# First layer's opening merged into its attention block, and the first group's row bound spread by a product with ones

## What is computed

```python
xn = layernorm(x, ln_x_g, ln_x_b)            # x: the context, 6404 rows
ln = layernorm(latents, ln_l_g, ln_l_b)      # latents: the (normed) residual, 1024 rows
q  = ln @ Wq
kv = concat([xn @ Wkv, ln @ Wkv])
qn, kn = rmsnorm(q, qn_g) * scale, rmsnorm(k, kn_g)
sim = where(mask, qn @ kn.T, max_neg)
out = softmax(sim) @ v @ Wout + bout
```

## Time and profile before

| | |
|---|---|
| median of three runs | 4295.99 us (4293.72 to 4296.5) |
| the profiled execution's own time | 4296.1 us |
| its span, first to last instruction | 4294.0 us |
| PE busy | 4024.4 us, 94% of the span |
| DVE busy | 3373.1 us, 79% |
| ACT busy | 3160.8 us, 74% |
| POOL busy | 417.7 us, 10% |

### The profile page before, as it was taken

How to read it: one execution, slowest core, us unless ns; L and a number is a source line. 1 busy time by engine, 2 the same in 40 slices (tenths; PEclk the granted TensorE clock), 3 DMA queues, 4 the chain that set the end, 5 groups by cost and what they waited for, 6 DMA issues and landing times. The chain is left out here.

```text
span 4294.0 us, 65601 instructions
## 1 busy us (share of the span) xinstructions
PE 4024.4 (94%) x25721; PEld 2648.7 (62%) x26161; DVE 3373.1 (79%) x5198; ACT 3160.8 (74%) x5109; POOL 417.7 (10%) x337
## 2 busy tenths in 40 slices
PE   3999999999999999999989799999999999999996
PEld 2666666666666666666657566666666666666664
DVE  5788888888887878878877677777777777777775
ACT  3888888888888888888864567676767676666662
POOL 3111111111111111111100000000000000000000
PEclk9999999999999999999989799999999999999997
DMA  1000000000000000000012000000000000000001
GB/s 40 1 1 16 1 5 13 1 17 1 5 13 1 17 1 6 11 1 18 1 34 92 5 1 17 1 17 1 17 1 5 13 3 15 1 16 1 15 1 44
DMA packets 29159, 50.25 MB, mean 12 GB/s; under 512 B 9118, under 2 KB 17574, under 8 KB 26790
## 3 DMA queue, kind: packets, MB, share of 16 engines
q1 hardware_dynamic: 26932, 45.85, 3.4%
q10 hardware_dynamic: 1922, 0.17, 0.0%
HBM read 45.15 MB, written 0.85 MB: 11 GB/s over the span
## 5 line engine op out<-in xcount | busy, mean ns | idle before, releaser
L824 DVE TENSOR_TENSOR a_probs_lo<-a_probs 128x1024 fp32r<-128x1024 f32 x1760 | 2126.2, 1222 | 562.3 <-ACT a_probs L637 253.4
L633 ACT ACTIVATE a_probs<-scores_ps,a_c_bias,a_k_rstd 128x512 f32<-128x512 f32 x1888 | 1311.9, 776 | 31.1 <-PE scores_ps L1180 30.8
L1205 PE MATMUL out_ps<-a_probs_lo,a_v 128*128 128x512 f32 x3520 | 1135.3, 443 | 0.0
L637 ACT ACTIVATE a_probs<-scores_ps,a_c_bias 128x1024 f32<-128x1024 f32 x816 | 867.7, 1112 | 113.4 <-PE scores_ps L1180 113.0
L1198 PE MATMUL out_ps<-a_probs,a_v 128*128 128x512 bf16 x3080 | 849.9, 389 | 85.2 <-issue 58.8
L1180 PE MATMUL scores_ps<-a_q_hi,a_k_hi 64*128 64x512 f32 x3520 | 790.9, 444 | 18.8 <-ACT a_probs L633 9.4
L1205 PEld LDWEIGHTS out_ps<-a_probs_lo,a_v 128*128 128x128 f32 x3520 | 658.7, 188 | 219.3 <-DVE a_probs_lo L824 0.5
L1180 PE MATMUL scores_ps<-a_q_lo,a_k_hi 64*128 64x512 f32 x3520 | 701.6, 393 | 0.0
L1180 PE MATMUL scores_ps<-a_q_hi,a_k_lo 64*128 64x512 f32 x3520 | 698.0, 391 | 0.0
L1198 PEld LDWEIGHTS out_ps<-a_probs,a_v 128*128 128x128 f16 x3520 | 272.4, 97 | 561.7 <-issue 304.8
L602 ACT ACTIVATE a_v<-proj_ps 128x256 f16<-128x256 f32 x448 | 172.2, 384 | 488.4 <-PE proj_ps L1112 488.2
(11 more groups left out here) (272 smaller groups left out, 3293.4 us busy)
## 6 DMA issues: line engine op xcount, KB each, us to landing
a_den<-a_inv_row SPq DMA_DIRECT2D x16, 1024.0 KB, 4.6
normed<-in_L_xattn_we_g SPq DMA_DIRECT2D x16, 256.0 KB, 2.8
m_gate_spread<-m_combine_row SPq DMA_DIRECT2D x8, 512.0 KB, 4.0
a_wkv_raw<-in_L_xattn_wkv_g SPq DMA_DIRECT2D x16, 128.0 KB, 2.1
a_wo_raw<-in_L_xattn_wo_g SPq DMA_DIRECT2D x16, 128.0 KB, 2.0
m_w_raw<-in_L_ffn_w1T SPq DMA_DIRECT2D x8, 256.0 KB, 4.3
m_w_raw<-in_L_ffn_w2T SPq DMA_DIRECT2D x8, 256.0 KB, 4.6
m_gate_spread<-m_combine_row SPq DMA_DIRECT2D x8, 256.0 KB, 5.8
```

The costliest lines, as they stand in the source:

```text
L633: ins = nc.scalar.activation(probs[:, pb, e * 512:(e + 1) * 512], scores[:, b, e * 512:(e + 1) * 512], ACT.Exp, bias=cbias[:, tile:tile + ...
L637: ins = nc.scalar.activation(probs[:, pb, :], scores[:, b, :], ACT.Exp, bias=cbias[:, 1:2] if last else cbias[:, 0:1])
L824: nc.vector.tensor_tensor(plow[:, idx % NPL, :], probs[:, idx % NB, :], p_hi[:, idx % NB], ALU.subtract).then_inc(plo_ready, 1)
L1205: nc.tensor.matmul(outs[:, e * 512:(e + 1) * 512], v32[:, c % 2, t, e, :], plow[:, idx % NPL, e * 512:(e + 1) * 512], start=False, stop=t ...
```

## The change

Layer 0's preparation block and the opening block of the kernel are gone; all their instructions now stand in the attention block's lists, woven into group 0's opening. The context is loaded in three parts (16, 20 and 15 tiles, a semaphore each) issued right behind X, the gates and the first weights, with nothing to wait for but the last four rows. It is placed in buffers that the steps use later (`probs`, `out_acc`); the transposed tiles go through a ring of five half-buffers instead of two, and their PSUM through four places. The latents' two low parts move from POOL to DVE. The order on each engine is written anew:

```diff
@@ DVE, layer 0 @@
+                    dve.wait_ge(B["loaded"], 48)
+                    ln_stats(dve, lstep, row_x, 0, QT, B["few"], var_ready, LATC)
+                    ctx_stats(0)
+                    ln_apply(dve, lstep, row_x, row_z, 0, QT, B["few"], rstd_ready, 1, LATC)
+                    ln_stats(dve, lstep, row_z, 0, QT, B["few"], var_ready, LATC)
                     constants()
                     wkv_low(0)
                     wq_low(0)
-                    q_var_of(0)
+                    ... (four small products of gains)
+                    ln_apply(dve, lstep, row_z, row_z, 0, QT, B["few"], rstd_ready, 3, LATC)
+                    dve.sem_inc(lat_ready, 1)
+                    ctx_norm(0, 2)
+                    ... (low parts of the latents' two jobs; mask copy)
+                    ctx_stats(1)
+                    ctx_stats(2)
                     v_low(0, 0)
                     k_var(0, 0)
+                    q_var_of(0)
                     k_low(0, 0)
+                    ctx_norm(1, 4)
+                    ... (mask bias)
                     q_scale(0)
                     v_low(0, 1)
                     k_var(0, 1)
+                    q_gained(0)
+                    ctx_norm(2, 5)
+                    lstep(nc.vector.tensor_copy(B["cms"][:, :, :], part[:, :, 6:8]))
                     k_low(0, 1)
-                    q_gained(0)
                     bound_norm(0)
-                    for n in range(2):
-                        q_low(0, n)
+                    q_low(0, 0)
+                    bound_here()
+                    q_low(0, 1)
+                    bound_everywhere()
                     v_low(0, 2)
                     k_var(0, 2)
                     k_low(0, 2)
+                    dve.wait_ge(xl_done, NCTXJ)
@@ PE, layer 0 @@
+                    turn(0, 1, 2, 3)
                     for b in range(2):
+                        pe.wait_ge(ll_done, b + 1)
                         project_q(0, b, None)
+                    turn(4, 5)
+                    project_kv(0, 0, 0, None)
+                    transpose_k(0, 0)
+                    ... (mask transpose)
+                    project_kv(0, 1, 0, None)
+                    turn(6, 7)
+                    transpose_k(0, 1)
+                    turn(8)
                     for b in range(2):
                         transpose_q(0, b, None)
+                    turn(9)
                     project_kv(0, 2, 0, None)
+                    turn(10)
+                    bound_turn()
+                    bound_spread()
                     transpose_k(0, 2)
+                    turn(11, 12)
...
-                project_kv(0, HEAD, 0, None)
+                if L == 0:
+                    turn(*range(13, len(jobs)))
+                    pe.wait_ge(tr_read, len(jobs))
                 pe.wait_ge(side_read, QSIDE0)
                 for n2 in range(2):
                     score(0, 0, 0, n2)
+                project_kv(0, HEAD, 0, None)
@@ POOL, layer 0 @@
+                    rstd(pool, QT, var_ready, rstd_ready, 1, LATC)
+                    ctx_rstd(0, 2)
+                    rstd(pool, QT, var_ready, rstd_ready, 3, LATC)
+                    lows(0, 2)
+                    ctx_rstd(1, 4)
+                    ctx_rstd(2, 5)
+                    k_rstd(0, 0)
+                    q_root(0)
+                    lows(2, 5)
+                    k_rstd(0, 1)
+                    lows(5, 7)
+                    lows(7, 9)
+                    bound_first()
+                    k_rstd(0, 2)
+                    lows(9, NCTXJ)
```

For group 0 of both layers the `PARTITION_ALL_REDUCE` is replaced. PE transposes `c_max` (128 by 2) to 2 by 128 in PSUM, DVE reduces each row to one number and puts the two on the diagonal of a 2 by 2 matrix, PE multiplies a 2 by 128 block of ones with it, which puts both numbers on all 128 partitions, DVE copies them out, and POOL takes the pow as before:

```diff
+                def bound_here():
+                    dve.wait_ge(b_turned, 1)
+                    nc.vector.tensor_reduce(diag2[:, 0:1], turned_ps, AX.X, ALU.max).then_inc(b_col, 1)
+                    dve.wait_ge(b_col, 1)
+                    nc.vector.tensor_scalar(diag2[:, 2:4], ident[0:2, 0:2], diag2[:, 0:1], None, ALU.mult).then_inc(b_diag, 1)
+
+                def bound_everywhere():
+                    dve.wait_ge(b_spread, 1)
+                    nc.vector.tensor_copy(call[:, :], spread_ps).then_inc(c_all, 1)
...
+                def bound_turn():
+                    pe.wait_ge(c_in_, 1)
+                    nc.tensor.transpose(turned_ps, cmx[:, :], ident[:, :]).then_inc(b_turned, 1)
+
+                def bound_spread():
+                    pe.wait_ge(b_ones, 1)
+                    pe.wait_ge(b_diag, 1)
+                    nc.tensor.matmul(spread_ps, ones2, diag2[:, 2:4], start=True, stop=True).then_inc(b_spread, 1)
```

More of the change, by code:

```diff
@@ new lines, in start_pool, with start_scalar @@
+        def start_pool(pool):
+            step = Steps(pool, made)
+            step(nc.gpsimd.memset(mhalf[:, :], -0.5))
+            step(nc.gpsimd.memset(phalf[:, :], 0.5))
+            step(nc.gpsimd.memset(ident[:, :], 0.0))
+            step(nc.gpsimd.affine_select(out=ident[:, :], in_=ident[:, :], compare_op=ALU.not_equal,
+                                         fill=1.0, base=0, pattern=[[-1, P]], channel_multiplier=1))
+        def start_scalar(act):
+            act.wait_ge(loaded, 48)
+            nc.scalar.activation(gates[:, :], gates[:, :], ACT.Tanh).then_inc(gated, 1)
@@ L410, in attention_layer, with raw, x_new, turn_ps @@
         den = sb("den", [P, GH, NQ])
+        if L == 0:
+            part = oacc[:, 0, 384:384 + 8 * (CTX_FULL + 1)].rearrange("p (t k) -> p t k", k=8)
+            early = probs[:, :, :].rearrange("p a (t d) -> p (a t) d", d=D)
+            late = oacc[:, 0, 0:384].rearrange("p (t d) -> p t d", d=D)
+            m8 = den[0:CTX_FULL, 1, 512:512 + P // 4].bitcast(U8)
+            mf = den[0:CTX_FULL, 1, 0:P]
+            m8r = den[0:CTX_REST, 1, 600:601].bitcast(U8)[:, 0:1]
+            NE_T = NB * NQ // D
+            YH = [Y[:, 0:4, :].rearrange("p a b -> p (a b)"), Y[:, 4:8, :].rearrange("p a b -> p (a b)")]
+            OH = [oacc[:, 1, 0:512], oacc[:, 1, 512:1024]]
+            RING = YH + OH + [Z[:, 4:8, :].rearrange("p a b -> p (a b)")]
+            NCTXJ = len(jobs) - 2
+            def raw(t):
+                return early[:, t, :] if t < NE_T else late[:, t - NE_T, :]
+            def x_new(i):
+                return OH[i] if i < 2 else RING[(i - 2) % len(RING)]
+            def turn_ps(i):
+                return scores[:, min(i // 2, 1), (i % 2) * 512:(i % 2 + 1) * 512]
+            def part_of(t):
+                return sum(t >= b for a, b in ln_parts)
         sums = sb("sums", [P, 2, GH * NQ // P])
@@ L580, in _, with lows, ctx_rstd @@
                     first(nc.gpsimd.memset(Y[:, :, :], 0.0))
-                q_root(0)
-                for k in range(2):
-                    k_rstd(0, k)
-                bound(0)
-                for k in range(2, HEAD + 1):
-                    k_rstd(0, k)
+                if L == 0:
+                    LATC = 52
+                    def lows(a, b):
+                        for m in range(a, b):
+                            hi, lo, w = job_out(*jobs[m + 2])
+                            pool.wait_ge(xh_done, m + 3)
+                            nc.gpsimd.tensor_tensor(lo, x_new(m + 2)[:, 0:w], hi.bitcast(F32), ALU.subtract).then_inc(xl_done, 1)
+                    def ctx_rstd(i, n):
+                        rstd(pool, ln_parts[i][1] - ln_parts[i][0], var_ready, rstd_ready, n, ln_parts[i][0])
+                    rstd(pool, QT, var_ready, rstd_ready, 1, LATC)
[13 more added lines that the diff above has]
+                    lows(9, NCTXJ)
+                    pool.wait_ge(xl_done, NCTXJ)
+                    first(nc.gpsimd.memset(Y[:, :, :], 0.0))
+                else:
+                    bound_first()
+                k_rstd(0, HEAD)
                 for g in range(NG):
@@ L713, in _, with turned @@
                 if L == 0:
+                    def turned(i):
+                        hi, lo, w = job_out(*jobs[i])
+                        if i >= 2 + len(RING):
+                            act.wait_ge(xl_done, i - 1 - len(RING))
+                        elif i - 2 in (2, 3):
+                            act.wait_ge(ll_done, i - 3)
+                        act.wait_ge(tr_done, i + 1)
+                        k = 2 if i < 2 else 0
+                        nc.scalar.activation(x_new(i)[:, 0:w], turn_ps(i)[:, 0:w], ACT.Identity, bias=col[:, k + 1:k + 2],
+                                             scale=col[:, k:k + 1]).then_inc(tr_read, 1)
+                        act.wait_ge(tr_read, i + 1)
+                        nc.scalar.activation(hi, x_new(i)[:, 0:w], ACT.Copy).then_inc(xh_done, 1)
+                    act.wait_ge(w_in, 16 * 11)
+                    for i in range(4):
+                        turned(i)
                     for b in range(2):
@@ L748, in _ @@
                 v_wide(0, 2)
+                if L == 0:
+                    for i in range(12, len(jobs)):
+                        turned(i)
                 bias_set(0)
```

318 lines of the change are left out of this document (145 added, 173 removed).

## The result

The changed kernel takes 4258.98 us (median of four runs, 4254.79 to 4259.28), the kernel before 4295.63 beside it (4293.72 to 4296.5): a ratio of 0.9913, 95% interval 0.9899 to 0.9927. The profiled execution took 4258.93. The forecast of 4256.5 was 2.5 us too low. This closeness comes in part from errors of both signs that cancel, as the traces show.

The account below looks back on a forecast made before the run. PE, busy 94%, was taken to bound the steps, leaving the stage edges, chiefly DVE's preparation chain and the bound. Gains of 29.8 + 11.9 less 1.1 and 1.0 made 39.6 us off 4296.1: 4256.5, range 4247 to 4267.

Parts of the forecast that it names:

- Layer 1's first `exp`: Layer 1's opening: with the new bound the exp comes at 2393.8 against 2405.76, 11.9 us earlier, bounds 11 to 13.
- PE, DVE and ACT all stand still during the all-reduce: From c_max to POOL's pow, 13.2 us in layer 0 and 13.4 in layer 1, both said to count in full.
- The ledger: Opening work added up duration by duration: DVE a solid chain to 61.5 us in layer 0, then the end through all engines.
- Layer 0's first `exp`: Merged opening of layer 0: exp at 77.8 us, 29.8 ahead of 107.55; gain between 26 and 36.
- the landing of the context: Start of layer 0: the context's first third, issued at about 3 us, lands at 9 us, bounds 8 and 12.
- The contention: DVE against POOL in layer 0's opening: each low part on POOL costs DVE 1.0 us; the pow costs nothing.
- Rival 1: POOL's pows block DVE too in the merged opening: exp at 83.4 to 87.8, total 4262 to 4266.5; chance 0.10.
- The charge for the moved projection: project_kv(0, HEAD) behind the two scores: costs 1.1 us in layer 0 and 1.0 in layer 1, bounds 0 and 1.6.
- The clock behind the first `exp`: Start of layer 0's steps: the clock rose 7 us after the first exp, and nothing changes in the work there.
- Rival 4: The low clock stays deep into group 0, each pair of steps taking some 4 us more: 4305 and more; chance 0.02.
- The sum: Whole kernel: 29.8 + 11.9 - 1.1 - 1.0 = 39.6 us off 4296.1, giving 4256.5.
- Checks that were named: Profile signs: no early all-reduce, 2 to 4.5 us to the pow, exp at 75 to 81, DVE busy over 90%.

Follow-up runs that it names:

- experiment 1: The kernel before with the product with ones in place of the first group's all-reduce in both layers, openings not merged: 4274.69 us, ratio 0.9954.
- Experiment 3: The changed kernel with the gates' two small loads issued behind the context, with their own semaphore: 4253.83 us, ratio 0.9903 to the kernel before.
- experiment 2: The changed kernel with the all-reduce put back for the first group of both layers: 4277.94 us, ratio 0.996 to the kernel before.
- experiment 4: The changed kernel with the context's low parts on POOL replaced by a memset of the same buffer: 4250.83 us in one run.
- experiment 5: The changed kernel with the fourth key projection back ahead of the first two scores in both layers: 4259.79 us, ratio 0.9917 to the kernel before.
- experiment 7: The changed kernel with 14 and 24 unused transposes in PE's idle stretches of layer 1's opening: 4259.2 us, ratio 0.9916 to the kernel before.
- experiment 6: Experiment 3's kernel with PE's turns 10 to 12 and ACT's query splits moved earlier in layer 0's opening: 4251.06 us, ratio 0.9898 to the kernel before.
- both of 8: Two kernels with experiment 6's order: POOL's clearing of Y moved later, 4248.57 us; the same plus 84 unused transposes on PE, 4245.18 us.
- late clearing: Experiment 6's kernel with POOL's clearing of Y moved behind the scale of the fourth group of keys: 4248.57 us, ratio 0.9892 to the kernel before.

## Why the prediction was right, and where its steps were wrong

- **Layer 1's first `exp`: right.** 11.9 us expected, 11.8 measured, and 8.3 us behind `q_square` where 8 were expected. The pieces of the bound took 2.1 us, inside their bounds of 2 to 4.5.
- **That PE, DVE and ACT all stand still during the all-reduce: a wrong reading, which the sum didn't use.** In the kernel before DVE works until 96.4 us, and PE has the fourth projection and two groups of scores to do, of which the last is this:

```profile
100.33 0.63 PE L1180 MATMUL scores_ps<-a_q_lo,a_k_hi 64*128 64x512 f32 x2
```

  In layer 1 the like ends at 2397.6. So the 13.2 and 13.4 us don't count in full: in experiment 1 the `exp` gains 7.2 us and 9.8. The ledger, worked out piece by piece, had 11.9 for layer 1 and needed the scores ahead of the projection for it.
- **Layer 0's first `exp`: 5.6 us too early in the forecast** (83.43 against 77.8). Along the ledger: part 0's statistics began at 13.31 and not at 9.0, which is 4.3 us and outside the bounds of 8 to 12; part 1's normalisation began 3.65 us late and took 7.24 us for 7.2 forecast; part 2's ended 3.6 late; the copy of the bound 4.0 late; POOL's last low part 5.2 late; the `exp` 5.6, of which 0.4 is the bias at 0.83 us. So the order of the ledger holds, and its durations add up, with errors both ways: the work between the two normalisations took 3.6 us and not 4.8, part 2's 8.0 and not 6.9. (Two slips are small: 2.14 us for 8 tiles is 0.27 each and not 0.257, though 16 tiles then took 4.19, and the third pass and part 0 add up to 26.3, not 26.5.) The step that failed is the one on the landing of the context. It put X and gates at 5.7 as before (7.63 measured) and the context at 9; it did not ask what the gates' small pieces do to a large load queued behind them. Experiment 3 gives that 2.6 of the 4.3 us. The other 1.7 stay open. This execution was even an early one: in the four others with the gates ahead (experiments 2, 4, 5, 7) the context landed at 13.93 to 14.02.
- **The contention: right in size.** 1.0 us per low part was charged, 0.85 to 0.9 measured. Part 2 met four low parts and not three.
- **Rival 1, pows that block DVE: fell.** The pow for part 2's rows (2.75 us from 42.30) and the query's (2.92 from 45.98) both lie beside DVE's work, and part 1's normalisation, which has the second of them and two low parts beside it, took the 7.2 us of two low parts alone; in experiment 4, with the pow and two clearings in place of the low parts beside it, it took 5.54 us, where 5.2 would be undisturbed (an estimate from the 16 tiles of part 0, 4.19 us with nothing on POOL beside them). By the rule of the Trainium skill (SBUF — State Buffer, "Who interferes with whom"), an exclusive lock of the shared ports for the whole instruction, that pow's 2.9 us would have come on top. The trace disagrees for the pow.
- **The charge for the moved projection: not seen in layer 0, and in layer 1 outweighed.** 2.1 us of loss behind the two first `exp` were put in. Behind layer 0's it is 540.8 us to the marker with the projection at either place, so nothing of the 1.1 shows. Behind layer 1's it is 1.3 us more than in experiment 5, near the 1.0 charged, but the clock has a part in that (next point). Against it stands what the old place costs: waits of 0.8 and 2.6 us for the scores. The whole move gains 0.7 us in layer 0 and 0.8 to 1.3 in layer 1.
- **The clock behind the first `exp`, taken to rise 7 us behind it as before: wrong, and it gave 1.9 us in layer 0.** From the first `exp` to layer 0's marker:

| kernel | clock at 1.00, us behind the first exp | exp to marker, us |
|---|---|---|
| before | 7.0 | 542.75 |
| experiment 2 | 4.8 | 541.7 |
| experiment 6 | 4.8 | 541.65 |
| experiment 4 | 2.9 | 541.35 |
| after | 1.5 | 540.85 |
| experiment 1 | already before it | 540.8 |

The projection stands ahead of the scores in the first and the last row and behind them in the others, and the time goes by the clock and not by it. The five executions left (experiments 3, 5, 7 and both of 8) have the clock up 0.5 us behind the `exp` or earlier, and 540.8 to 540.9 us. Layer 1 shows the same, read in windows of 0.5 to 2 us: 237.4 us with the rise 6.0 us behind its `exp` (before), 236.8 at 3.2 (after), 236.1 at 1.6 (late clearing), 235.7 at 1.0 (experiment 1) and 235.5 at 0.4 (experiment 5). Rival 4 asked about the clock in the other direction only.
- **The sum, as measured against forecast gains.** Layer 0: 24.1 + 1.9 = 26.0 for 29.8 - 1.1 = 28.7, so 2.7 too little. Layer 1: 12.3 for 11.9 - 1.0 = 10.9, so 1.4 more. The two expert stages: 0.7 + 0.8 lost, nothing forecast, and within their scatter. Together 2.7 too little in the span; the profiled execution's time missed the forecast by 2.4. That it is no more is in part luck: without the clock's 1.9 us and with the charge left out, layer 0 alone would have missed by 5.7.
- **What is open:** 1.7 us of the landing, and why the clock rises when it does: in experiment 6 PE worked without a break from 70.8 to 75.1 us and the clock rose only at about 79.2.
- **Checks that were named:** no all-reduce in either opening: seen. DVE over 90% busy from 9 to 61 us: 46.88 of 52 us, just 90%, since it waited 3.16 us for the context. The `exp` at 75 to 81: missed, by the landing. Normalisations of 7 us each: 7.2 and 8.0. From `c_max` to the pow 2 to 4.5 us: 2.1 in layer 1, but 5.9 in layer 0, where the new bound's steps stand on DVE behind the 3.10 us wait for ACT's split of the queries; experiment 6 removed that. Of the three signs of being wrong two showed (the context after 12 us, a wait of more than 2 us before the second key item) and one did not (the pace behind 120 us: the shift of 26.0 us stays).

## What to carry to other kernels

When two preparations are merged, follow each queue from its first entry. A load that held back no large one where it stood (two gates of 1 KB) can hold back the one that now stands behind it, and on a solid chain every microsecond of that comes out at the end. An operation in which an engine stands for 13 us costs what nothing else covers, not 13 us: here 7.2 and 9.8 at the first `exp`, since PE had work beside it in both layers, and, once other items queue up behind it on the same engine, their wait too. Write down, too, where the clock stands when the dense part begins: here that was worth up to 1.9 us in either layer, beyond the shortening itself, and inside layer 1's opening 2.8.

## What the runs showed of the hardware

- Two loads in small pieces ahead of a 1 MB load in one queue: 6% busy DMA engines and 1 GB/s over 2 us, against 97% and 216 GB/s with them behind it.
- A clearing of 128x1024 on GpSimd slowed a tensor-scalar of 128x59 on VectorE from 0.25 to 0.83 us, so that it ended just behind the clearing; two clearings of 128x512 and a pow of 128x16 under the long normalisation cost it little (5.54 us for an estimated 5.2), and a subtraction of 128x512 costs it 0.85 to 0.9 us.
- The granted clock rose to 1.00 in layer 1's opening with 14 and 24 transposes in it, and fell to 0.50 again in the idle stretch behind them; with the gaps filled it held from 2334 to 2354 us. In two executions without transposes there (experiments 4 and the late clearing) it rose too, some 10 and 11 us later in the opening. The query projection's 24 matmuls then took 2.9 us rather than 5.4.
- A partition all-reduce has a record of 0.37 us on GpSimd and takes 13.2 to 13.4 us from the maximum to the next instruction's start in an idle queue.
